# Wide cross attention of a two-layer decoder: keys and values folded into the weights, heads side by side, the norm inside the loop

## The chip, the cores and the metric

The kernel runs on one core of a Trainium2 chip. The metric is the device time of one execution in microseconds. Three runs of the kernel before took 2298.8, 2303.5 and 2313.93 us: median 2303.5 us.

## What is computed

Two decoder layers on x (4 batches, 512 tokens, 128 features), each with self attention, cross attention and experts, a layer norm behind each. The change is in the cross attention of the second layer, with 16 heads of width 64 over a context of 77 rows of 128 features for each batch:

```
q = einsum('bqm,mhd->bqhd', x, Wq) + bq
k = einsum('bkm,mhd->bkhd', ctx, Wk) + bk
v = einsum('bkm,mhd->bkhd', ctx, Wv) + bv
attn = softmax(einsum('bqhd,bkhd->bhqk', q / sqrt(64), k), axis=-1)
out  = einsum('bqhd,hdm->bqm', einsum('bhqk,bkhd->bqhd', attn, v), Wo) + bo
x = layernorm(x + out)
```

Everything here is float32.

## The kernel before, in words

The program is written by engine. Each function opens a block in which the engines run their own lists of instructions and wait on counting semaphores; between blocks all engines meet. Constants: P = 128, B = 4 batches, S = 512 tokens of a batch, QT = 4 tiles of 128 tokens in a batch, NT = 16 tiles in all, KC = 77 context rows, H = 16 heads, PAIRS = 8 pairs of heads. Lasting tiles are X (tokens on partitions), XT (its transpose, features on partitions) and CTT (the context transposed). PSUM has ps_s (four banks of 512 columns), ps_t (two), ps_v and ps_f (one each).

The stage named e has three parts.

- **Operands** (first block of `wide_cross_attention`). SP loads four weights of 512 KB and four biases; PE waits for all of them. For each pair of heads PE makes keys (L1685, 308 columns: 4 batches of 77) and half a batch of values (L1690, 512 columns); DVE writes them out with their biases (L1702 twice, L1707).
- **The loop** (second block), 32 turns: a batch and a pair of heads in each, for all 512 tokens. `project` (L1721) makes the queries, which ACT takes out (L1836); `score` (L1728) multiplies four token tiles by the keys of two heads side by side (154 columns); `lessen` on DVE takes maxima (L1785) and subtracts them (L1788); ACT takes the exponential (L1830); `norm` on DVE sums (L1795), inverts (L1797) and scales (L1799); `turn` on PE makes eight transposes of 77 columns (L1739), ACT takes them out (L1854); `weigh` (L1750) multiplies the values; DVE takes the heads out (L1807); `add` (L1758) multiplies by Wo and sums over the pairs in ps_f. The order on each engine is written out by hand. PE's turn is: score of the pair two ahead, turn, project three ahead, add of the pair before, weigh. DVE's turn is: lessen two ahead, norm one ahead, take the heads out. The first batch and the last are written out, the two between run in a hardware loop.
- **The norm** (`finish`, tag e). A block of its own: it transposes the output back to tokens (L948), adds X (L1008), takes statistics (L846, L849), POOL computes the inverse root (L857, L859), DVE applies it (L866), and PE and ACT rebuild XT (L959, L983).

The next stage's first instruction is a load of the router's weights. `lessen`, `take`, `turn` and `score` also name inner functions of other stages; those are not touched.

Of the kernel before, what the change touches and what calls it, by code (L numbers as in the profile page):

```python
# [5 lines left out]
F32 = mybir.dt.float32  # L6
# [5 lines left out]
P = 128  # L12
# [19 lines left out]
CLIP = 16  # L32
EPS = 1e-5
# [1595 lines left out]

def wide_cross_attention(c, tag, wq, bq, wk, bk, wv, bv, wo, bo, OT):  # L1630

    nc = c.nc
    with ExitStack() as own:
        WQ, WK, WV = (c.sb(f"{tag}_W{n}", [P, H * HD64], F32, own) for n in "qkv")
        WO = c.sb(f"{tag}_Wo", [P, PAIRS, P], F32, own)
        BQ = c.sb(f"{tag}_BQ", [P, PAIRS], F32, own)
        BK = c.sb(f"{tag}_BK", [P, PAIRS], F32, own)
        BV = c.sb(f"{tag}_BV", [KC, H * HD64], F32, own)
        BO = c.sb(f"{tag}_BO", [P, 1], F32, own)
        KB = c.sb(f"{tag}_KB", [P, PAIRS, B, 2, KC], F32, own)  # L1640
# [3 lines left out]
        SC = c.sb(f"{tag}_SC", [P, 2, 2 * QT, KC], F32, own)
        PR = c.sb(f"{tag}_PR", [P, 2, 2 * QT, KC], F32, own)
        PT = c.sb(f"{tag}_PT", [SROWS, 2, S], F32, own)
        CT = c.sb(f"{tag}_CT", [P, S], F32, own)
        M = c.sb(f"{tag}_M", [P, 2 * QT], F32, own)
        DEN = c.sb(f"{tag}_DEN", [P, 2 * QT], F32, own)
        RDEN = c.sb(f"{tag}_RDEN", [P, 2 * QT], F32, own)  # L1650
        (s_w, s_zero, s_scaled, s_kproj, s_kout, s_vproj, s_vout, s_vb, proj, q_out, scores, maxed, lessened, exped, summed,
         inverted, normed, turned, taken, products, heads_out, added, s_ot) = (
            c.sem(f"{tag}_{n}") for n in
            ("w", "zero", "scaled", "kproj", "kout", "vproj", "vout", "vb", "proj", "q_out", "scores", "maxed", "lessened",
             "exped", "summed", "inverted", "normed", "turned", "taken", "products", "heads_out", "added", "ot"))
        N_W = 16 * 8

        with nc.Block() as block:
            @block.sync
            def _(sp):  # L1660
                for dst, src in ((WQ, wq), (WK, wk), (WV, wv)):
                    sp.dma_start(dst[:, :], src.rearrange("m h d -> m (h d)")).then_inc(s_w, 16)
                sp.dma_start(WO[:, :, :], wo.rearrange("(g e) d n -> (e d) g n", e=2)).then_inc(s_w, 16)
                sp.dma_start(BQ[:, :], bq.rearrange("(g e) d -> (e d) g", e=2),
                             allow_slow_non_contiguous=True).then_inc(s_w, 16)
                sp.dma_start(BK[:, :], bk.rearrange("(g e) d -> (e d) g", e=2),
                             allow_slow_non_contiguous=True).then_inc(s_w, 16)
# [12 lines left out]
            def _(pe):  # L1680
                pe.wait_ge(s_w, N_W)
                for p in range(PAIRS):
                    if p >= 2:
                        pe.wait_ge(s_kout, 2 * (p - 1))
                    nc.tensor.matmul(c.ps_s[:, p % 2, 0:B * KC], WK[:, p * P:(p + 1) * P], c.CTT[:, :],  # L1685
                                     start=True, stop=True).then_inc(s_kproj, 1)
                    b, half = p // 2, p % 2
                    if p >= 2:
                        pe.wait_ge(s_vout, p - 1)
                    nc.tensor.matmul(c.ps_t[0:KC, half, :], c.CTT[:, b * KC:(b + 1) * KC], WV[:, half * 512:(half + 1) * 512],  # L1690
                                     start=True, stop=True).then_inc(s_vproj, 1)
# [510 lines left out]
```

## Time and profile before

| what | us |
|---|---|
| median of three runs (lowest, highest) | 2303.5 (2298.8, 2313.93) |
| the profiled execution, first to last instruction | 2295.7 |
| stage e: operands | 27.6 |
| stage e: loop | 167.9 |
| stage e: norm function | 16.7 |
| PE, DVE, ACT, POOL busy over the span | 1810.9, 1433.0, 1046.3, 119.8 |

The span is measured inside one profiled execution; no separate duration is given for that execution, and the runs' times, taken on other executions, are 3.1 to 18.2 us above it. The table is read by stage: only the three rows on stage e belong to code that changes. Engine times say how long an engine had an instruction in it; a matmul's end is modelled, so overlapping matmuls are shown longer than the steps between them. A float32 matmul stands as two entries, a float32 transpose as one. PEclk is TensorE's granted clock: 1.00 is 2.4 GHz, 0.50 is 1.2 GHz.

### The profile page before, as it was taken

The page shows a single profiled execution, that of the slowest core. Times are in us where ns is not written, and L with a number is a line of the kernel's source. Part 1 is how long each engine was busy: PE and PEld are TensorE (multiplying, and loading weights), DVE is VectorE, ACT ScalarE, POOL GpSimd, SP SyncE. Part 2 cuts the span into 40 slices and gives each one's busy share as a digit, 9 for nine tenths or more (in the row PEclk, how much of TensorE's full clock was granted, in tenths as well). Part 3 has the DMA queues.
Part 4 walks back from the last instruction along what each step waited for, and adds up shares of the span by engine and source line. Part 5 has one row for each costly group of instructions (what it writes and reads, how often), then busy time and mean ns, then how long its engine had stood idle before and what let it go on. Part 6 is the DMA issues. An engine that isn't in the chain of part 4 may idle for free. (4 is left out here: it accounts for less than half of the span.)

```text
span 2295.7 us, 33834 instructions
## 1 busy us (share of the span) xinstructions
PE 1810.9 (79%) x9702; PEld 1004.4 (44%) x9702; DVE 1433.0 (62%) x4803; ACT 1046.3 (46%) x1972; POOL 119.8 (5%) x244
## 2 busy tenths in 40 slices
PE   3288774684169559699985999999999959998997
PEld 2144442453013223477762444444444425555664
DVE  7398886565368446333336777777767757875445
ACT  3288881471026346243432555666665513441221
POOL 2000003001000000100001000000000020000000
PEclk7599996796569779699997999999999978997999
DMA  1543200510531230100001000000000010000000
GB/s 57 80 44 37 28 0 22 72 21 22 90 35 18 24 42 1 31 10 19 26 2 37 1 1 1 1 1 1 0 1 1 1 43 1 0 1 21 15 21 25
DMA packets 56587, 48.93 MB, mean 21 GB/s; under 512 B 11742, under 2 KB 51922, under 8 KB 56479
## 3 DMA queue, kind: packets, MB, share of 16 engines
q1 hardware_dynamic: 56479, 47.67, 12.8%
q8 instruction: 47, 0.77, 0.1%
q14 instruction: 61, 0.50, 0.1%
HBM read 38.54 MB, written 8.91 MB: 21 GB/s over the span
## 5 line engine op out<-in xcount | busy, mean ns | idle before, releaser
L1431 PE MATMUL ps_s<-d_KZ,d_Q 128*128 128x512 f32 x512 | 265.4, 601 | 16.2 <-issue 6.8
L1579 ACT ACTIVATE d_PR<-d_PR,d_NM 128x512 f32<-128x512 f32 x256 | 184.7, 721 | 190.0 <-DVE d_NM L1510 189.5
L556 DVE TENSOR_REDUCE c_NM<-ps_t 128x1 f32<-128x512 f32 x256 | 170.0, 689 | 96.8 <-PE ps_t L436 95.1
L1506 DVE CUSTOM_DVE_ANT_0 d_PR<-ps_s,d_BH 128x512 f32<-128x512 f32 x256 | 176.3, 689 | 61.6 <-PE ps_t L1439 44.7
L2116 DVE SCALAR_TENSOR_TENSOR X<-ps_t,GATE,X 128x128 f32<-128x128 f32 x272 | 76.6, 345 | 183.7 <-PE ps_t L2041 183.7
L436 PE MATMUL ps_t<-KX,QX 96*128 (+1 forms) x256 | 108.1, 427 | 105.3 <-DVE c_IB L574 46.2
L618 ACT ACTIVATE c_PT<-ps_s 128x1024 f32<-128x1024 f32 x128 | 130.3, 1023 | 126.8 <-PE ps_s L459 124.8
L1439 PEld LDWEIGHTS ps_t<-ident,d_PR 128*128 128x128 f32 x1024 | 121.4, 141 | 150.6 <-issue 132.4
L1586 ACT ACTIVATE d_PT<-ps_t 128x512 f32<-128x512 f32 x256 | 149.6, 585 | 50.7 <-PE ps_t L1439 49.1
L761 ACT ACTIVATE a_PR<-a_PR,a_NM 128x128 f32<-128x128 f32 (+3 forms) x256 | 129.8, 555 | 78.5 <-DVE a_NM L742 78.5
L1439 PE MATMUL ps_t<-ident,d_PR 128*128 128x128 f32 x1024 | 156.5, 276 | 10.0 <-ACT d_PT L1586 8.1
L671 PE MATMUL ps_t<-ident,a_PR 128*128 128x128 f32 x640 | 115.8, 290 | 46.7 <-ACT a_PT L685 37.7
L2078 ACT ACTIVATE f_HT<-ps_s,f_BE 128x512 f32<-128x512 f32 x128 | 87.7, 687 | 127.8 <-PE ps_s L2031 127.1
L2031 PE MATMUL ps_s<-XT,g_W 128*128 128x512 f32 x288 | 132.6, 604 | 1.1 <-DVE g_HT L2095 1.1
L1518 DVE TENSOR_SCALAR d_PR<-d_PR,d_RDEN 128x512 f32<-128x512 f32 x256 | 124.7, 487 | 9.0
L2041 PEld LDWEIGHTS ps_t<-f_W,f_HT 128*128 128x128 f32 x1024 | 119.2, 192 | 14.8 <-issue 14.6
L1451 PE MATMUL ps_v<-d_PT,d_VB 128*64 128x512 f32 x512 | 116.9, 598 | 5.6 <-ACT d_PT L1586 4.8
L2041 PE MATMUL ps_t<-f_W,f_HT 128*128 128x128 f32 x1024 | 119.3, 275 | 0.0
L2031 PE MATMUL ps_s<-XT,f_W 128*128 128x512 f32 x256 | 116.6, 599 | 0.0
L671 PEld LDWEIGHTS ps_t<-ident,a_PR 128*128 128x128 f32 x640 | 70.6, 142 | 96.1 <-ACT a_PT L685 48.0
L2076 ACT ACTIVATE g_GT<-ps_s 128x512 f32<-128x512 f32 x72 | 43.0, 597 | 141.8 <-PE ps_s L2031 141.8
L436 PEld LDWEIGHTS ps_t<-KX,QX 96*128 (+1 forms) x256 | 25.0, 98 | 184.3 <-issue 105.3
(306 smaller groups left out, 3182.2 us busy)
## 6 DMA issues: line engine op xcount, KB each, us to landing
QX<-split_parts SPq DMA_DIRECT2D x108, 128.0 KB
KX<-split_parts SPq DMA_DIRECT2D x72, 128.0 KB
f_W<-in_L_ffn_w SPq DMA_DIRECT2D x16, 256.0 KB, 3.1
split_parts<-a_PARTS SPq DMA_DIRECT2D x8, 384.0 KB, 10.4
split_parts<-c_PARTS SPq DMA_DIRECT2D x8, 384.0 KB, 10.8
g_W<-in_L_ffn_w SPq DMA_DIRECT2D x24, 128.0 KB, 2.2
split_parts<-b_PARTS SPq DMA_DIRECT2D x4, 384.0 KB, 10.5
X<-in_x SPq DMA_DIRECT2D x4, 256.0 KB
```

Source lines behind the costliest of these rows:

```text
L436: nc.tensor.matmul(c.ps_t[:, i % 2, :], QX[0:SROWS, bass.ds(head, 1), qt * P:(qt + 1) * P], KX[0:SROWS, bass.ds(head, 1), :], start=True, ...
L556: nc.vector.tensor_reduce(NM[:, qt, j:j + 1], c.ps_t[:, i % 2, :], AX.X, ALU.max, negate=True).then_inc(maxed, 1)
L618: nc.scalar.activation(PT[:, half, j, :, :], c.ps_s[:, 2 * (j % 2):2 * (j % 2) + 2, :], ACT.Exp).then_inc(exped, 1)
L671: last = nc.tensor.transpose(c.ps_t[:, qt % 2, kt * P:(kt + 1) * P], PR[:, j % 2, qt, kt * P:(kt + 1) * P], c.ident[:, :])
L761: nc.scalar.activation(PR[:, j % 2, qt, 0:k], PR[:, j % 2, qt, 0:k], ACT.Exp, bias=NM[:, j % 2, qt:qt + 1]).then_inc(exped, 1)
L1431: nc.tensor.matmul(c.ps_s[:, qt % 2, :], Q[:, p % 2, qt * P:(qt + 1) * P], KZ[:, p % 2, i % 2, :], start=True, stop=True).then_inc(scores, 1)
L1439: mm = nc.tensor.transpose(c.ps_t[:, qt % 2, kt * P:(kt + 1) * P], PR[:, i % 2, qt, kt * P:(kt + 1) * P], c.ident[:, :])
L1506: nc.vector.tensor_tensor_reduce(out=PR[:, h % 2, qt, :], in0=c.ps_s[:, qt % 2, :], in1=BH[:, h, S - P - qt * P:2 * S - P - qt * P], scale ...
L1579: nc.scalar.activation(PR[:, h % 2, qt, :], PR[:, h % 2, qt, :], ACT.Exp, bias=NM[:, h % 2, qt:qt + 1], accum_out=DEN[:, h % 2, qt:qt + 1] ...
L1586: nc.scalar.activation(PT[:, i // 2 % 2, i % 2, :, qt * P:(qt + 1) * P], c.ps_t[:, qt % 2, :].rearrange("p (k q) -> p k q", q=P), ACT.Copy ...
L2031: nc.tensor.matmul(c.ps_s[:, ch, :], W[:, (ch % CH) * P:(ch % CH + 1) * P], c.XT[:, b * S:(b + 1) * S], start=True, stop=True).then_inc(s_ ...
L2041: mm = nc.tensor.matmul(c.ps_t[:, b % 2, q * P:(q + 1) * P], HT[:, b % 2, ch, q * P:(q + 1) * P], W2[i][:, ch, :], start=(ch == 0), stop=( ...
```

## The change

`wide_cross_attention` and `finish` for stage e are replaced by three functions. For each head h, `wide_operands` folds Wq[h] and the keys into A[h] = Wq[h] K[h]^T / 8 (128 features by 308 context rows), and the values and Wo[h] into U (context rows by 128 features). `flat_cross` then multiplies XT by A directly, with no queries, and the probabilities by U, with no product with Wo. The query bias becomes a row CP that is added by a second matmul, in three bfloat16 parts against ones.

A turn is now half of a token tile's heads: 8 heads of 77 columns side by side, 616 columns padded to 640, which makes five transposes of 128 columns. There are again 32 turns, all written out. The exponential is taken in place. The scaling by 1/sum is `normalise` on GpSimd, L1853 of the new kernel. The output bias is added to X on GpSimd before the loop. The output of a tile is added to X by DVE (L1982), and statistics, scaling and the new XT of a batch are done within the turns of the next batch; the last batch's follow the loop.

The diff, cut; removed lines are those of the function shown above.

```diff
-def wide_cross_attention(c, tag, wq, bq, wk, bk, wv, bv, wo, bo, OT):
...
+def flat_operand_tiles(c, tag, ctx):
+    A = c.sb(f"{tag}_A", [P, B, H, KC], F32, ctx)
+    CP = c.sb(f"{tag}_CP", [NPART, H, B, KC], BF16, ctx)
+    U = c.sb(f"{tag}_U", [P, B, 2 * CHUNKS, P], F32, ctx)
+    return A, CP, U
...
+def wide_operands(c, tag, wq, bq, wk, bk, wv, bv, wo, A, CP, U):
...
+                for dst, src in ((WK, wk), (WV, wv), (WQ, wq)):
                     sp.dma_start(dst[:, :], src.rearrange("m h d -> m (h d)")).then_inc(s_w, 16)
                 sp.dma_start(WO[:, :, :], wo.rearrange("(g e) d n -> (e d) g n", e=2)).then_inc(s_w, 16)
+                for dst, src in ((BQ, bq), (BK, bk), (BV, bv)):
+                    sp.dma_start(dst[:, :], pairs(src), allow_slow_non_contiguous=True).then_inc(s_w, 16)
...
+                for p in range(PAIRS):
+                    if p >= 2:
+                        pe.wait_ge(s_kout, p - 1)
+                    nc.tensor.matmul(c.ps_s[:, p % 2, 0:K2], WK[:, p * P:(p + 1) * P], c.CTT[:, :],
+                                     start=True, stop=True).then_inc(s_k, 1)
+                    if p >= 2:
                         pe.wait_ge(s_vout, p - 1)
+                    nc.tensor.matmul(c.ps_s[:, 2 + p % 2, 0:K2], WV[:, p * P:(p + 1) * P], c.CTT[:, :],
+                                     start=True, stop=True).then_inc(s_v, 1)
+                    mm = nc.tensor.transpose(c.ps_t[:, p // 4, (p % 4) * P:(p % 4 + 1) * P], WQ[:, p * P:(p + 1) * P],
+                                             c.ident[:, :])
+                    if p % 4 == 3:
+                        mm.then_inc(s_wqt, 1)
+                pe.wait_ge(s_bq, 2)
+                pe.wait_ge(s_kout, PAIRS)
+                for p in range(PAIRS):
+                    mm = nc.tensor.matmul(c.ps_f[0:H, 0:K2], BQH[:, p * H:(p + 1) * H], KT[:, p, :],
+                                          start=(p == 0), stop=(p == PAIRS - 1))
+                mm.then_inc(s_c, 1)
+                pe.wait_ge(s_wqtout, 2)
+                pe.wait_ge(s_vout, PAIRS)
+                for p in range(PAIRS):
+                    if p >= 2:
+                        pe.wait_ge(s_aout, 2 * (p - 1))
+                    for e in range(2):
+                        r = slice(e * HD64, (e + 1) * HD64)
+                        mm = nc.tensor.matmul(scored(2 * p + e), WQT[r, p, :], KT[r, p, :], start=True, stop=True)
+                    mm.then_inc(s_a, 1)
+                    if p == 1:
+                        pe.wait_ge(s_split, 1)
+                    if p >= 2:
+                        pe.wait_ge(s_uout, 2 * (p - 1))
+                    for e in range(2):
+                        r = slice(e * HD64, (e + 1) * HD64)
+                        mm = nc.tensor.matmul(valued(2 * p + e), WO[r, p, :], VT[r, p, :], start=True, stop=True)
+                    mm.then_inc(s_u, 1)
+                pe.wait_ge(s_aout, H)
+                pe.wait_ge(s_zero, 2)
+                for g in range(B * 2):
+                    b, half = g // 2, g % 2
+                    if g == 0:
+                        pe.wait_ge(s_uout, H)
+                    if g >= 2:
+                        pe.wait_ge(s_tout, g - 1)
+                    for i in range(CHUNKS):
+                        mm = nc.tensor.transpose(c.ps_s[:, 2 * (g % 2) + i // 4, (i % 4) * P:(i % 4 + 1) * P],
+                                                 UT[:, b, half, i * P:(i + 1) * P], c.ident[:, :])
+                    mm.then_inc(s_t, 1)
...
+                for h in range(H):
+                    act.wait_ge(s_a, h // 2 + 1)
+                    nc.scalar.activation(A[:, :, h, :], scored(h).rearrange("p (b k) -> p b k", b=B),
+                                         ACT.Copy).then_inc(s_aout, 1)
+                for g in range(B * 2):
+                    act.wait_ge(s_t, g + 1)
+                    nc.scalar.activation(U[:, g // 2, (g % 2) * CHUNKS:(g % 2 + 1) * CHUNKS, :].rearrange("p i d -> p (i d)"),
+                                         c.ps_s[:, 2 * (g % 2):2 * (g % 2) + 2, :].rearrange("p a n -> p (a n)")[:, 0:W],
+                                         ACT.Copy).then_inc(s_tout, 1)
...
+                for h in range(H):
+                    dve.wait_ge(s_u, h // 2 + 1)
+                    nc.vector.tensor_copy(UT[:, :, h // 8, (h % 8) * KC:(h % 8 + 1) * KC],
+                                          valued(h).rearrange("p (b k) -> p b k", b=B)).then_inc(s_uout, 1)
...
+def flat_cross(c, tag, A, CP, U, bo, pre=None):
...
+                pool.wait_ge(s_w, n_w)
+                for b in range(B):
+                    x = c.X[:, b * QT:(b + 1) * QT, :]
+                    nc.gpsimd.tensor_tensor(x, x, BO[:, :].rearrange("p (a d) -> p a d", a=1).broadcast_to([P, QT, P]),
+                                            ALU.add).then_inc(s_bias, 1)
...
+                def normalise(h):
+                    pool.wait_ge(inverted, h + 1)
+                    nc.gpsimd.tensor_tensor(
+                        heads(PR[:, h % RING, 0:HH * KC]), heads(PR[:, h % RING, 0:HH * KC]),
+                        RDEN[:, h % 2, :].rearrange("p (h a) -> p h a", a=1).broadcast_to([P, HH, KC]),
+                        ALU.mult).then_inc(normed, 1)
+                for h in range(HALVES):
+                    normalise(h)
+                    if h % (2 * QT) == 3 and h > 3:
+                        for k in range(norms):
+                            rstd((h // (2 * QT) - 1) * norms + k)
+                for k in range(norms):
+                    rstd((B - 1) * norms + k)
...
+                def score(h):
+                    t, half = h // 2, h % 2
+                    b = t // QT
+                    if h >= 2:
+                        pe.wait_ge(lessened, h - 1)
+                    for q in range(2):
+                        g = slice(half * HH + 4 * q, half * HH + 4 * q + 4)
+                        dst = c.ps_s[:, 2 * (h % 2) + q, 0:4 * KC]
+                        nc.tensor.matmul(dst, c.XT[:, t * P:(t + 1) * P], A[:, b, g, :].rearrange("p h k -> p (h k)"),
+                                         start=True, stop=False)
+                        mm = nc.tensor.matmul(dst, ONES[:, :], CP[:, g, b, :], start=False, stop=True)
                     mm.then_inc(scores, 1)
+                def turn(h):
+                    pe.wait_ge(normed, h + 1)
+                    if h >= 1:
+                        pe.wait_ge(taken, h)
+                    for i in range(CHUNKS):
+                        mm = nc.tensor.transpose(c.ps_t[:, i // 4, (i % 4) * P:(i % 4 + 1) * P],
+                                                 PR[:, h % RING, i * P:(i + 1) * P], c.ident[:, :])
                     mm.then_inc(turned, 1)
+                def weigh(h):
+                    t, half = h // 2, h % 2
+                    pe.wait_ge(taken, h + 1)
+                    if half == 0 and t >= 2:
+                        pe.wait_ge(summed_x, t - 1)
+                    for i in range(CHUNKS):
+                        mm = nc.tensor.matmul(output(t), PT[:, h % 2, i * P:(i + 1) * P], U[:, t // QT, half * CHUNKS + i, :],
+                                              start=(half == 0 and i == 0), stop=(half == 1 and i == CHUNKS - 1))
+                    mm.then_inc(weighed, 1)
+                def back(b):
+                    pe.wait_ge(s_n, QT * (b + 1))
+                    for i in range(QT):
+                        src = c.X[:, b * QT + i, :] if pre is None else R2[:, i, :]
+                        mm = nc.tensor.transpose(c.ps_t[:, 0, i * P:(i + 1) * P], src, c.ident[:, :])
+                    mm.then_inc(s_back, 1)
+                pe.wait_ge(s_ones, 1)
+                pe.wait_ge(s_pad, 1)
+                score(0)
+                score(1)
+                for h in range(HALVES):
+                    if h % (2 * QT) == 6 and h > 6:
+                        pe.wait_ge(taken, h)
+                        back(h // (2 * QT) - 1)
+                        pe.wait_ge(s_xt, h // (2 * QT))
+                    turn(h)
+                    if h + 2 < HALVES:
+                        score(h + 2)
+                    weigh(h)
+                back(B - 1)
...
+                def exp(h):
+                    act.wait_ge(lessened, h + 1)
+                    nc.scalar.activation(PR[:, h % RING, 0:HH * KC], PR[:, h % RING, 0:HH * KC], ACT.Exp).then_inc(exped, 1)
+                def take(h):
+                    act.wait_ge(turned, h + 1)
+                    if h >= 2:
+                        act.wait_ge(weighed, h - 1)
+                    nc.scalar.activation(PT[:, h % 2, :], c.ps_t[:, :, :].rearrange("p a n -> p (a n)")[:, 0:W],
+                                         ACT.Copy).then_inc(taken, 1)
...
+                for h in range(HALVES):
+                    if h % (2 * QT) == 6 and h > 6:
+                        columns(h // (2 * QT) - 1)
+                    take(h)
+                    if h + 2 < HALVES:
+                        exp(h + 2)
...
+                def lessen(h):
+                    dve.wait_ge(scores, h + 1)
+                    m = M[:, h % 2, :].rearrange("p (a m) -> p a m", a=2)
+                    nc.vector.reduce_max(m, score_banks(h), AX.X).then_inc(maxed, 1)
+                    dve.wait_ge(maxed, h + 1)
+                    if h >= RING:
+                        dve.wait_ge(turned, h - RING + 1)
+                    nc.vector.tensor_tensor(
+                        PR[:, h % RING, 0:HH * KC].rearrange("p (a m k) -> p a m k", a=2, k=KC), score_banks(h),
+                        M[:, h % 2, :].rearrange("p (a m b) -> p a m b", a=2, b=1).broadcast_to([P, 2, 4, KC]),
+                        ALU.subtract).then_inc(lessened, 1)
+                def total(h):
+                    dve.wait_ge(exped, h + 1)
+                    nc.vector.reduce_sum(DEN[:, h % 2, :], heads(PR[:, h % RING, 0:HH * KC]), AX.X).then_inc(summed, 1)
+                    dve.wait_ge(summed, h + 1)
+                    if h >= 2:
+                        dve.wait_ge(normed, h - 1)
+                    nc.vector.reciprocal(RDEN[:, h % 2, :], DEN[:, h % 2, :]).then_inc(inverted, 1)
+                def add(t):
+                    dve.wait_ge(weighed, 2 * t + 2)
+                    if t == 0:
+                        dve.wait_ge(s_bias, B)
+                    nc.vector.tensor_tensor(c.X[:, t, :], c.X[:, t, :], output(t), ALU.add).then_inc(summed_x, 1)
...
+                lessen(0)
+                lessen(1)
+                total(0)
+                for h in range(HALVES):
+                    if h + 2 < HALVES:
+                        lessen(h + 2)
+                    if h + 1 < HALVES:
+                        total(h + 1)
+                    if h % 2 == 0 and h >= 2:
+                        add(h // 2 - 1)
+                    if h > 3 and h % (2 * QT) in (2, 3, 4, 5)[:1 + norms] and h >= 2 * QT:
+                        layer(h // (2 * QT) - 1, h % (2 * QT) - 2)
+                add(NT - 1)
+                for step in range(1 + norms):
+                    layer(B - 1, step)
+                done.wait(dve)
...
-            wide_cross_attention(c, "e", *(a[f"L1_xattn_{n}"] for n in ("Wq", "bq", "Wk", "bk", "Wv", "bv", "Wo", "bo")), OT)
-            finish(c, "e", "dm", OT=OT)
+            A, CP, U = flat_operand_tiles(c, "e", own)
+            wide_operands(c, "e", *(a[f"L1_xattn_{n}"] for n in ("Wq", "bq", "Wk", "bk", "Wv", "bv", "Wo")), A, CP, U)
+            flat_cross(c, "e", A, CP, U, a["L1_xattn_bo"])
         with ExitStack() as own:
             GATE = c.sb("GATE1", [P, NT, NE + 1], F32, own)
```

The order on PE, where the scores are made in the loop. Before (a stretch of the hardware loop; L1728 score, L1739 turn, L1721 project, L1758 add, L1750 weigh):

```order
L1739 MATMUL ps_t<-ident,e_PR 77x128 x8
L1721 MATMUL ps_s<-XT,e_Wq 128x512
L1758 MATMUL ps_f<-e_CT,e_Wo 128x512
L1750 MATMUL ps_v<-e_PT,e_VB 64x512 x2
L1728 MATMUL ps_s<-e_KB,e_Q 128x154 x4
L1739 MATMUL ps_t<-ident,e_PR 77x128 x8
```

The same place in the changed kernel (L1886 turn, L1876 and L1878 score, L1896 weigh):

```order
L1886 MATMUL ps_t<-ident,e_PR 128x128 x5
L1876 MATMUL ps_s<-e_A,XT 128x308
L1878 MATMUL ps_s<-e_CP,e_ONES 128x308
L1876 MATMUL ps_s<-e_A,XT 128x308
L1878 MATMUL ps_s<-e_CP,e_ONES 128x308
L1896 MATMUL ps_v<-e_U,e_PT 128x128 x5
L1886 MATMUL ps_t<-ident,e_PR 128x128 x5
```

The score of two turns ahead stood before the turn's transposes; now it stands behind them, and ahead of the weighing.

The order on DVE in the loop. Before (L1785 and L1788 lessen, L1795 to L1799 norm, L1807 heads out):

```order
L1785 TENSOR_REDUCE e_M<-ps_s 128x8
L1788 TENSOR_TENSOR e_SC<-ps_s,e_M 128x616
L1795 TENSOR_REDUCE e_DEN<-e_PR 128x8
L1797 RECIPROCAL e_RDEN<-e_DEN 128x8
L1799 TENSOR_TENSOR e_PR<-e_PR,e_RDEN 128x616
L1807 COPY e_CT<-ps_v 128x512
```

Now (L1961 and L1965 lessen, L1972 and L1976 total, L1982 add of a finished tile, every second turn):

```order
L1961 TENSOR_REDUCE e_M<-ps_s 128x8
L1965 TENSOR_TENSOR e_PR<-ps_s,e_M 128x616
L1972 TENSOR_REDUCE e_DEN<-e_PR 128x8
L1976 RECIPROCAL e_RDEN<-e_DEN 128x8
L1961 TENSOR_REDUCE e_M<-ps_s 128x8
L1965 TENSOR_TENSOR e_PR<-ps_s,e_M 128x616
L1972 TENSOR_REDUCE e_DEN<-e_PR 128x8
L1976 RECIPROCAL e_RDEN<-e_DEN 128x8
L1982 TENSOR_TENSOR X<-X,ps_v 128x128
```

The scaling has left DVE, and the copy of 512 columns has become an addition of 128; maxima and subtraction of a later turn still come ahead of the sums of an earlier one.

## Rows read from the trace of the kernel before

**Rows 1.** Windows by stage: length, busy us per engine (count), PEclk, DMA share, GB/s.
```profile
1867.90:1895.50 27.60, 14.03 (x32) 5.70 (x32) 13.74 (x25) 0.00 (x0) 8.65 (x3) 0.73 0.31 88
1895.50:2063.40 167.90, 162.05 (x768) 92.85 (x768) 130.05 (x196) 72.65 (x100) 0.00 (x0) 0.96 0.00 1
2063.40:2080.10 16.70, 6.70 (x32) 4.42 (x32) 11.77 (x52) 3.05 (x5) 5.06 (x8) 0.71 0.00 0
```

**Rows 2.** Timeline, one turn of the loop: start us, us, instruction, [idle before <-releaser].
```profile
1977.41 1.31 PE L1728 MATMUL ps_s<-e_KB,e_Q 128*128 x8
...
1978.57 1.04 PE L1739 MATMUL ps_t<-ident,e_PR 128*77 128x128 f32 x8
1978.77 0.80 DVE L1785 TENSOR_REDUCE e_M<-ps_s 128x8 f32<-128x616 f32 x1 [0.54 <-PE ps_s L1728]
...
1979.69 0.80 DVE L1788 TENSOR_TENSOR e_SC<-ps_s,e_M 128x616 f32<-128x616 f32 x1
...
1980.40 0.78 DVE L1795 TENSOR_REDUCE e_DEN<-e_PR 128x8 f32<-128x616 f32 x1
...
1981.22 0.20 DVE L1797 RECIPROCAL e_RDEN<-e_DEN 128x8 f32<-128x8 f32 x1
...
1981.25 1.08 PE L1750 MATMUL ps_v<-e_PT,e_VB 96*64 96x512 f32 x4
1981.46 0.80 DVE L1799 TENSOR_TENSOR e_PR<-e_PR,e_RDEN 128x616 f32<-128x616 f32 x1
...
1982.26 1.31 PE L1728 MATMUL ps_s<-e_KB,e_Q 128*128 x8
```

**Rows 3.** Timeline, the stage's weights and operands.
```profile
1867.90 0.33 SPq L1662 DMA_DIRECT2D e_Wq<-in_L_xattn_Wq  x1
...
1870.38 3.83 SPq L1666 DMA_DIRECT2D e_BK<-in_L_xattn_bk  x1
...
1878.85 1.40 PE L1685 MATMUL ps_s<-CTT,e_Wk 128*128 128x308 f32 x2 [11.84 <-DMA e_BO<-in_L_xattn_bo]
...
1880.36 1.11 DVE L1702 TENSOR_SCALAR e_KB<-ps_s,e_BK 64x308 f32<-64x308 f32 x2 [1.35 <-PE ps_s L1685]
...
1883.63 0.68 PE L1685 MATMUL ps_s<-CTT,e_Wk 128*128 128x308 f32 x2
...
1894.53 0.69 DVE L1707 TENSOR_TENSOR e_VA<-ps_t,e_BV 77x512 f32<-77x512 f32 x1
```

**Rows 4.** Timeline, end of the loop and the separate norm function.
```profile
2065.35 0.69 DVE L1008 TENSOR_TENSOR e_fR<-X,ps_s 128x512 f32<-128x512 f32 x1 [3.19 <-PE ps_s L948]
...
2066.98 0.38 DVE L849 BATCH_NORM_AGGREGATE e_fMV<-e_fST 128x2 f32<-128x6 f32 x4
...
2067.45 0.23 POOL L857 TENSOR_SCALAR e_fRS<-e_fMV 128x4 f32<-128x4 f32 x1 [190.77 <-DVE e_fMV L849]
...
2071.32 0.60 ACT L983 ACTIVATE XT<-ps_t 128x512 f32<-128x512 f32 x1 [7.26 <-PE ps_t L959]
...
2079.28 0.60 ACT L983 ACTIVATE XT<-ps_t 128x512 f32<-128x512 f32 x1 [0.99 <-PE ps_t L959]
```

**Rows 5.** Groups by line on POOL, whole span: op, shapes xcount | busy us, mean ns.
```profile
L365 POOL COPY VG<-c_VN 128x32 f32 x56 | 11.4, 209 | 278.5 <-PE ps_v L476 278.5
...
L1673 POOL MEMSET e_KB<- 128x4928 f32 x1 | 4.2, 4204 | 3.2 <-POOLq L903 3.2
...
L367 POOL COPY VG<-b_VB 96x8 f32 x14 | 2.6, 186 | 81.5 <-PE ps_v L1236 81.5
```

**Rows 6.** Timeline, PE early in the loop.
```profile
1907.64 0.59 PE L1728 MATMUL ps_s<-e_KB,e_Q 128*128 128x154 f32 x1 [2.91 <-DVE e_SC L1788]
```

**Rows 7.** Windows early in the loop, columns as in the first group.
```profile
1903.50:1906.50 3.00, 1.24 (x8) 1.00 (x8) 2.34 (x4) 1.13 (x2) 0.00 (x0) 1.00 0.00 0
1907.00:1913.00 6.00, 5.36 (x18) 4.25 (x18) 3.32 (x6) 1.94 (x3) 0.00 (x0) 0.50 0.00 0
1914.00:1926.00 12.00, 12.00 (x67) 7.49 (x64) 9.22 (x14) 4.57 (x7) 0.00 (x0) 1.00 0.01 1
```

More of the change, by code:

```diff
@@ L32 @@
 CLIP = 16
+CHUNKS = 5
 EPS = 1e-5
@@ L1644, in wide_cross_attention @@
[L1644 to L1655, printed above, removed]
@@ L1709, in ahead @@
-        def ahead(b, p, k):
-            return (b, p + k) if p + k < PAIRS else (b + 1, p + k - PAIRS)
-        def more(p, k, last):
-            return not last or p + k < PAIRS
-        with nc.Block() as block:
+                split = Chain(s_split)
+                dve.wait_ge(s_w, 16 * 7)
+                dve.wait_ge(s_zero, 1)
+                for e in range(2):
+                    r = slice(e * HD64, (e + 1) * HD64)
+                    nc.vector.tensor_scalar(BQH[r, e::H + 2], BQ[r, :], ISQ64, None, ALU.mult).then_inc(s_bq, 1)
@@ L1754, in add @@
-                def add(b, p):
-                    wait(pe, heads_out, b * PAIRS + p + 1)
-                    if p == 0:
-                        wait(pe, s_ot, b)
-                    nc.tensor.matmul(c.ps_f[:, :], WO[:, p, :], CT[:, :], start=(p == 0), stop=(p == PAIRS - 1)).then_inc(added, 1)
-                def batch(b, first, last):
-                    if first:
-                        project(b, 0)
-                        project(b, 1)
-                        score(b, 0)
-                        project(b, 2)
-                        score(b, 1)
-                    for p in range(PAIRS):
-                        if more(p, 2, last):
-                            score(*ahead(b, p, 2))
-                        turn(b, p)
-                        if more(p, 3, last):
-                            project(*ahead(b, p, 3))
-                        if not (first and p == 0):
-                            add(*((b, p - 1) if p else (b - 1, PAIRS - 1)))
-                        weigh(b, p)
@@ L1803, in take_heads @@
-                def take_heads(b, p):
-                    n = b * PAIRS + p
-                    dve.wait_ge(products, n + 1)
-                    dve.wait_ge(added, n)
-                    nc.vector.tensor_copy(CT[:, :], c.ps_v[:, :]).then_inc(heads_out, 1)
-                def batch(b, first, last):
-                    wait(dve, products, b * PAIRS)
-                    nc.vector.tensor_copy(VB[:, :], VA[:, bass.ds(b, 1), :].rearrange("p a n -> p (a n)")).then_inc(s_vb, 1)
-                    if first:
-                        lessen(b, 0)
-                        norm(b, 0)
-                        lessen(b, 1)
-                    for p in range(PAIRS):
-                        if more(p, 2, last):
-                            lessen(*ahead(b, p, 2))
-                        if more(p, 1, last):
-                            norm(*ahead(b, p, 1))
-                        take_heads(b, p)
```

262 lines of the change are left out of this document (133 added, 129 removed).

## The prediction

> **What bounds the kernel now.** I read the windows by stage first, because one stage of several changes. Stage e takes 27.6 us for its operands, 167.9 for its loop and 16.7 for its norm function, 212.2 us in all [rows 1]. In the loop PE is busy 162.05 of 167.9 us, DVE 130.05, ACT 72.65, POOL not at all: PE bounds it. In the operands and the norm nothing is full; there the order of waits counts. Then I read one turn in the timeline: from score to score 4.85 us (1977.41 to 1982.26) [rows 2]. The reader should see in it that DVE's maxima start while PE is still in its transposes: score stands ahead of the transposes on PE, so DVE works on a later pair of heads while PE turns an earlier one. Over 32 turns, 4.85 us make 155 us; the rest of the loop is its start.
>
> **What the change takes away.** Queries, the product with Wo, the copy of the heads (DVE), the copy of queries (ACT), the scaling on DVE, and the separate norm function. Of a turn's work PE keeps five transposes of eight, 5/8 of 1.04 = 0.65 us; the score, two float32 products of 308 columns at 0.68 each from start to end [rows 3], 1.36 us; two bfloat16 products of 308 columns; and the weighing, five products of 128 columns, about 1.1 us (640 columns by 0.68/308, less overlapping ends). The trace has no bfloat16 product of this form: it costs at least nothing and at most one of the two entries of the float32 one, 0.34 us; I take 0.1 for both beyond the overlap, nearer to nothing since the ends shown overlap. Together 3.2 us for PE. DVE keeps 0.80 + 0.80 + 0.78 + 0.20 [rows 2], half of an addition of 128 columns and an eighth of a batch's norm, about 3.1 us. Against 4.85 that looks like a gain of 1.7 us a turn. It is not the sum, for what follows.
>
> **The order makes a chain.** PE now issues turn(h), score(h+2), weigh(h). turn(h) waits for POOL's scaling of h, which waits for DVE's total(h). DVE issues total(h) behind lessen(h+1), which waits for score(h+1), which PE issues behind turn(h-1). So turn(h-1), score(h+1), lessen(h+1), total(h), normalise(h), turn(h) follow each other with nothing beside them but the weighing and the ACT copies. Queued behind the waiting turn on PE is the score of two turns ahead, and DVE waits for that: the two stages of prefetch buy nothing. Before, score of two ahead waited for no transposes.
>
> The price of a turn, at 2.4 GHz: transposes 0.65; scores 1.36 + 0.1 = 1.46; DVE from the start of the maxima to the point where the scaling can start 2.69 (1978.77 to 1981.46) [rows 2]; scaling p; handovers PE to DVE and POOL to PE, 0.15 together (DVE to POOL took 0.09, from 2067.36 to 2067.45 [rows 4]).
>
> **The scaling on GpSimd, p.** No POOL row has two inputs of this length. A copy of 32 columns takes 209 ns, of 8 columns 186 [rows 5]: 0.96 ns a column over a fixed 0.18 us. For 616 columns one input is 0.77 us. With two inputs I take twice the cost per column, 1.36 us. Below, the memset, which reads nothing, costs 4204/4928 = 0.85 ns a column: 0.53 and a tenth for the start, 0.63 us. Above, three times the copy's slope: 1.95 us. The copy is the nearest row, since it reads and writes as the scaling does; DVE's 0.80 for the same work is another engine's. The Trainium skill, "GPSIMD Engine Reference", section "Elementwise — side-by-side cycle accounting", speaks against this move: two inputs cost GpSimd 1.96 times what they cost VectorE. By that, an estimate of 1.96 x 0.80 = 1.57 us would make the sum 6 us longer; no run here shows it yet.
>
> With p = 1.36 a turn is 0.65 + 1.46 + 2.69 + 1.36 + 0.15 = **6.3 us** at 2.4 GHz, and PE is idle for some 3 us of it. At 1.2 GHz transposes and scores double, which gives 8.4 us; DVE, ACT and POOL do not change.
>
> **The clock.** In the first turns of the loop before, PE stood idle 2.91 us for DVE [rows 6]; from 1903.5 to 1906.5 it was busy 1.24 us and the clock was 1.00, and from 1907 to 1913 it was at 0.50 although PE was busy 5.36 of 6 us; unbroken work followed and it was 1.00 again from 1914 on [rows 7]. The new turn contains such an idle stretch every time, and behind it come just the transposes and scores that lie on the chain; the rise comes, if at all, in the weighing, which does not. I take the middle of the two levels, 7.35 us a turn. The Trainium skill, "TensorE: Matmul & The Clock Gate", section "What's actually happening", puts it so that the slow level is the default and activity releases it; the trace agrees, and the rule's extreme, a loop that never leaves 1.2 GHz, is a rival below.
>
> **Loop and norm.** Start: two scores at the low clock 5.8, lessen(1) and total(0) 2.7, scaling and handover 1.5: 10.0 us. The four bias additions on POOL and the load of the bias lie beside that. 30 turns x 7.35 = 220.5. The last turn has no score ahead: 1.5. Behind it the last transposes, copy and weighing, 2.5, and one batch's norm, from the addition to the end of the new XT: 2065.35 to 2071.92 = 6.6 [rows 4]. Sum 241.1 us against 167.9 + 16.7 = 184.6 [rows 1]: **+56.5**. The norms of the first three batches I cost at nothing: DVE is idle for more than 3 us of a turn and POOL for some 6; if the chain were gone they would cost DVE about 0.3 us a turn.
>
> **Operands.** Before, 10.95 us until the last bias landed (1867.90 to 1878.85), then 16.7 us of products [rows 3]. Now: loads 13.0, since a third bias is scattered by columns, which cost SP 3.83 us to issue for one such, where a row load stood; I take 2 of 0 to 4 us. Keys, values and turned Wq, 8 x 1.2 = 9.6, and 1.7 for the start at half clock, where the first product shows 1.40 for 0.68: 11.3. The bias row, eight products in turn and the first split, 5.1. A and U: 32 products of half height. If the two halves of a pair run side by side, DVE's two copies set it, 1.11 a pair as the two of 308 columns [rows 3]: 8.9 us. If not, PE does, with four at 0.51: 16.4. The nearest row is the weighing before, whose two column halves run together (four entries of 512 columns in 1.08 us [rows 2]), so I take 8.9. Turning U: eight groups at 0.75 for ACT's 640 columns (512 take 0.60 [rows 4]) and a start: 6.8. Handover 0.8. Sum 45.9 against 27.6: **+18.3**, from 16 to 28.
>
> **The sum.** 2295.7 + 56.5 + 18.3 = 2370.5 us for the profiled execution's span. The median of the runs lies 7.8 us above the span of before; with the same around it the median is **2378 us**, 3.2% slower.
>
> **Rivals.**
> - Clock at 1.00 all through. For it: the idle stretch is only half of a turn, and weighing joins on to transposes and scores. Against it: [rows 6, 7]. 6.3 us a turn: 2378 - 30 x 1.05 = 2346 us.
> - Clock at 0.50 all through. For it: 5.36 busy of 6 us did not raise it at once [rows 7]. Against it: then PE works some 6 us of 8.4 without a break, where those 6 us held pauses. 2378 + 31 = 2410 us.
> - A cheap scaling, 0.63 us, together with the high clock: 5.6 us a turn, 2324 us, within 1%. Needs the lower bound of two costs.
> - The other side: the chain does not close, and DVE's 3.1 us set the turn. The place is DVE's wait for the score behind total(h): it would need score(h+1) done before turn(h-1) has been released, which the order forbids. 2378 - 30 x 4.25 = 2250 us, faster. The point at which it decides: the operands, start and end take 45.9 + 20.6 us, so the stage equals its old 212.2 us at 4.86 us a turn.
> - The change doing less than it says: GpSimd's scaling is certainly in the list, so this only concerns the halves of A and U; serial halves add 7.5 us to any case.
>
> **Chances.** Alternating clock 0.50, high 0.27, low 0.13, cheap and high 0.05, no chain 0.05. The range takes in the first three with the scaling's ends (18 us either way) trimmed: 2325 to 2415 us. A measurement of this kernel tells about 1% from no change, 23 us. Slower by more 0.90, within 0.05, faster 0.05.
>
> **What would show it.** In the changed kernel's profile: DVE's maxima waiting for PE's scores in nearly every turn; PE's transposes waiting for the scaling about 3 us; 6.3 to 8.4 us between two groups of transposes; 1.36 us for the scaling; PEclk between 0.5 and 1.0 in the loop; the operands 44 to 56 us long; about 10 us between the last scaling and the router's load. The forecast fails if turns are below 5.6 us, if the scaling is far outside 0.6 to 2 us, or if the idle stretch leaves the clock alone.

## The result, and the profile after

The changed kernel takes **2385.4 us** (median; 2377.0 to 2395.0), the kernel before 2302.9 us in the same comparison: 1.035 times as long, 95% interval 1.032 to 1.039. The forecast was 2378 us and slower. The profiled execution of the new kernel has a span of 2393.2 us and is its slowest run, so its stages are compared by their lengths and not by the span. Of the page of the new kernel:

```profile
span 2393.2 us, 33578 instructions
...
PE 1842.1 (77%) x9665; PEld 1041.4 (44%) x9718; DVE 1385.4 (58%) x4754; ACT 1035.7 (43%) x1970; POOL 155.9 (7%) x281
...
PEclk7699995896588989899969999999999865766999
```

The last row is the granted clock in 40 slices: it stands at 5 to 7 tenths in the four slices of this stage's loop. The windows by stage, to be held against [rows 1] (length; busy us, with counts, of PE, PEld, DVE, ACT and POOL; PEclk, DMA share, GB/s):

```profile
1876.00:1920.00 44.00, 30.52 (x160) 19.88 (x160) 13.79 (x32) 16.29 (x34) 0.55 (x3) 0.83 0.18 49
1920.00:2175.00 255.00, 192.57 (x688) 124.75 (x688) 94.18 (x192) 47.86 (x68) 49.03 (x46) 0.63 0.00 1
```

From the first weight load to the router's load, stage e took 212.2 us before and takes 299.1 now, +86.9: operands 44.0 against 27.6, loop with norms 255.1 against 167.9 + 16.7. The other 10.6 us by which this execution's span is longer lie in stages that the change doesn't touch (8.1 ahead, 2.5 behind); in the kernels of the experiments, which are the same up to this stage, it starts anywhere from 1866 to 1878 us. DVE has only 94.18 us of work in the loop, where it had 130.05 and 11.77, and PE's 192.57 is more than its old 162.05 only because its clock stood at 0.63 on average instead of 0.96: the same 688 entries take 125.1 us at a clock of 0.92 in the kernel with the total ahead of lessening, below (1918.0 to 2060.7).

One turn at the high clock (start us, us, instruction, [idle before <-releaser]), in place of [rows 2]:

```profile
2040.13 0.74 PE L1886 MATMUL ps_t<-ident,e_PR 128*128 128x128 f32 x5 [1.34 <-ACT XT L1939]
...
2040.70 0.69 PE L1876 MATMUL ps_s<-e_A,XT 128*128 128x308 f32 x2
...
2042.27 0.30 PE L1878 MATMUL ps_s<-e_CP,e_ONES 3*128 3x308 bf16 x1
...
2042.50 1.38 PE L1896 MATMUL ps_f<-e_U,e_PT 128*128 128x128 f32 x10
2042.61 0.80 DVE L1961 TENSOR_REDUCE e_M<-ps_s 128x8 f32<-128x616 f32 x1 [3.87 <-PE ps_s L1878]
...
2045.26 1.22 POOL L1853 TENSOR_TENSOR e_PR<-e_PR,e_RDEN 128x616 f32<-128x616 f32 x1 [5.23 <-DVE e_RDEN L1976]
2046.53 0.53 PEld L1886 LDWEIGHTS ps_t<-ident,e_PR 128*128 128x128 f32 x5 [2.83 <-POOL e_PR L1853]
2046.53 0.77 PE L1886 MATMUL ps_t<-ident,e_PR 128*128 128x128 f32 x5 [2.65 <-POOL e_PR L1853]
```

Read it as a ladder: transposes (2040.13), score (2040.70 to 2042.57), DVE (2042.61), scaling (2045.26), transposes (2046.53). Each starts where the one before ends, and the brackets tell the same: every engine waits for the one ahead, PE 2.65 us, DVE 3.87, POOL 5.23. (The first line names ACT's XT as what ended its wait, since a new batch starts there; XT was copied by 2039.43, and the scaling ended at 2040.03, so this wait too is for the scaling.) Before, DVE's maxima had begun beside PE's transposes. At the low clock a turn is longer:

```profile
1938.08 1.33 PE L1886 MATMUL ps_t<-ident,e_PR 128*128 128x128 f32 x5 [1.52 <-POOL e_PR L1853]
...
1942.54 0.80 DVE L1961 TENSOR_REDUCE e_M<-ps_s 128x8 f32<-128x616 f32 x1 [5.80 <-PE ps_s L1878]
...
1945.19 1.22 POOL L1853 TENSOR_TENSOR e_PR<-e_PR,e_RDEN 128x616 f32<-128x616 f32 x1 [7.16 <-DVE e_RDEN L1976]
...
1946.46 1.33 PE L1886 MATMUL ps_t<-ident,e_PR 128*128 128x128 f32 x5 [1.53 <-POOL e_PR L1853]
```

From 1938.08 to 1946.46 are 8.38 us; transposes and score take 4.46 instead of 2.48 and nothing else changes. DVE's maxima wait for the score 32 times, every turn (us in all, times, the longest):

```profile
DVE e_M L1961 <- PE ps_s L1878: 153.0, 32, 9.7
```

### The profile page after: what moved, and what is told of

Its sections match the earlier page's. It is cut to its first block and busy times, and to the rows that moved or that the text cites. A ratio compares the mean times of both kernels' runs of the same rounds, so it can differ in the third digit from the quotient of the medians.

```text
span 2393.2 us, 33578 instructions
## 1 busy us (share of the span) xinstructions
PE 1842.1 (77%) x9665; PEld 1041.4 (44%) x9718; DVE 1385.4 (58%) x4754; ACT 1035.7 (43%) x1970; POOL 155.9 (7%) x281
## 5 line engine op out<-in xcount | busy, mean ns | idle before, releaser
L1961 DVE TENSOR_REDUCE e_M<-ps_s 128x8 f32<-128x616 f32 x32 | 25.6, 800 | 153.0 <-PE ps_s L1878 153.0
```

## The experiments

The comparisons are against the kernel before (2302.0 us for the first four, 2300.7 for the next four, 2302.6 for the last). "The stage" is the length from the first weight load to the router's load, 212.2 us before and 299.1 in the change. Lengths of turns are those within a batch; where a new batch starts, a turn can be longer.

**Score ahead of the transposes, on PE.**

```diff
-                    turn(h)
                     if h + 2 < HALVES:
                         score(h + 2)
+                    turn(h)
```

> Only PE's order in the loop changes: score(h+2) stands ahead of turn(h). Theory (the order closes a chain through turn, score, lessen, total and scaling): the chain then runs over two turns, weighing and the wait for ACT's copy now on it; two turns cost about 2.4 (transposes, copy, weighing) + 1.5 (score) + 2.7 (DVE) + 1.4 (scaling and handovers) = 8.0 us, so 4.0 to 4.3 us a turn instead of 7.67, and the clock stays up since PE works 3.2 of them: 2385 - 30 x 3.5 = 2275 to 2285 us, below the kernel before. Rival (GpSimd's scaling or the engines' own work bounds the turn): no engine has less to do, so 2375 to 2390 us.

Measured: 2295.4 us, ratio 0.998 (0.996 to 0.999); the stage 207.0 us; a turn 4.57 us. The timeline:

```profile
1992.40 0.70 ACT L1932 ACTIVATE e_PT<-ps_t 128x640 f32<-128x640 f32 x1 [2.89 <-PE ps_t L1886]
...
1993.16 1.38 PE L1896 MATMUL ps_f<-e_U,e_PT 128*128 128x128 f32 x10 [0.79 <-ACT e_PT L1932]
...
1994.36 1.22 POOL L1853 TENSOR_TENSOR e_PR<-e_PR,e_RDEN 128x616 f32<-128x616 f32 x1 [3.36 <-DVE e_RDEN L1976]
1994.38 0.68 PE L1876 MATMUL ps_s<-e_A,XT 128*128 128x308 f32 x2
...
1996.17 0.77 PE L1886 MATMUL ps_t<-ident,e_PR 128*128 128x128 f32 x5
```

The chain is gone: the scaling (1994.36 to 1995.58) is over before PE wants it at 1996.17. Two lines swapped take 92 us off the stage. It stays above the 2275 to 2285 us that were expected since PE's own row now sets the turn: it stands idle 0.79 us for ACT's copy before each weighing, and the score takes 1.8 us.

**Total ahead of lessening, on DVE.**

```diff
+                    if h + 1 < HALVES:
+                        total(h + 1)
                     if h + 2 < HALVES:
                         lessen(h + 2)
-                    if h + 1 < HALVES:
-                        total(h + 1)
```

> Only DVE's order changes: total(h+1) stands ahead of lessen(h+2). Chain theory: the scaling of h+1 runs beside score(h+2), the chain is turn, score, lessen, exponential, total, scaling over two turns, 0.65 + 1.5 + 1.6 + 0.7 + 1.0 + 1.4 = 6.9 us for two; DVE has 3.1 us of work and about 0.8 of waiting for the exponential in each turn, so about 4.0 to 4.5 us a turn: 2275 to 2290 us. Rival (work of the engines): 2375 to 2390 us.

Measured: 2276.7 us, 0.989 (0.987 to 0.990); the stage 186.7 us; turns of 3.56 and 3.74 us.

```profile
1992.76 1.22 POOL L1853 TENSOR_TENSOR e_PR<-e_PR,e_RDEN 128x616 f32<-128x616 f32 x1 [2.34 <-DVE e_RDEN L1976]
...
1992.88 1.38 PE L1896 MATMUL ps_v<-e_U,e_PT 128*128 128x128 f32 x10
1992.98 0.80 DVE L1961 TENSOR_REDUCE e_M<-ps_s 128x8 f32<-128x616 f32 x1 [0.30 <-PE ps_s L1878]
...
1994.09 0.71 PE L1886 MATMUL ps_t<-ident,e_PR 128*128 128x128 f32 x5
...
1995.40 0.80 DVE L1972 TENSOR_REDUCE e_DEN<-e_PR 128x8 f32<-128x616 f32 x1 [0.59 <-ACT e_PR L1926]
```

The scaling now runs beside the weighing and PE has no gap at 1994.09; DVE waits 0.30 us for the score and not 3.87. So the same chain can be opened on either engine, and DVE's side is the better one: PE's order stays transposes, score, weighing, so that the score runs while ACT makes its copy (1991.53 to 1992.22) and PE finds it done at 1992.88. The turns are below the 4.0 to 4.5 us expected; the median is within the 2275 to 2290 expected, since turns that hold a part of a norm take longer, two of them 5.43 us.

**The scaling on DVE, orders as in the change.**

```diff
-                    nc.gpsimd.tensor_tensor(
...
                     nc.vector.reciprocal(RDEN[:, h % 2, :], DEN[:, h % 2, :]).then_inc(inverted, 1)
+                    dve.wait_ge(inverted, h + 1)
+                    nc.vector.tensor_tensor(
+                        heads(PR[:, h % RING, 0:HH * KC]), heads(PR[:, h % RING, 0:HH * KC]),
...
```

> The scaling is back on DVE, behind the reciprocal; all orders stay. Chain theory: the chain loses 1.22 + 0.1 us and gains 0.80, so 7.95 instead of 8.38 us a turn at the low clock and 6.0 instead of 6.4 at the high one, minus 13 us: about 2372 us, still 3% above the kernel before. Rival (GpSimd's scaling is what makes the change slow): most of the 82 us go, 2300 to 2320 us.

Measured: 2362.5 us, 1.026 (1.024 to 1.029); the stage 270.8 us; turns of 5.97 us at the high clock, 7.55 and 7.92 with the low one in them.

```profile
2043.98 0.80 DVE L1970 TENSOR_TENSOR e_PR<-e_PR,e_RDEN 128x616 f32<-128x616 f32 x1
...
2044.84 0.77 PE L1878 MATMUL ps_t<-ident,e_PR 128*128 128x128 f32 x5 [1.30 <-DVE e_PR L1970]
...
2047.35 0.80 DVE L1953 TENSOR_REDUCE e_M<-ps_s 128x8 f32<-128x616 f32 x1 [2.37 <-PE ps_s L1870]
```

DVE still waits for the score behind the transposes. In the chain GpSimd costs 28 us of the stage and 23 of the median, where 13 were expected. Its longer instruction and the handover make 0.46 us a turn at either clock (6.43 against 5.97, 8.38 against 7.92), 14 us; most of the rest are turns at the low clock, of which this kernel has fewer: its mean turn is 6.85 us against 7.67. GpSimd is not what makes the kernel slow.

**PE kept busy.** This kernel does work that nobody needs: five more products of 308 columns behind each weighing, where PE was idle.

```diff
                     weigh(h)
+                    for _ in range(5):
+                        nc.tensor.matmul(c.ps_t[:, 1, P:P + B * KC], c.ident[:, :], c.CTT[:, :], start=True, stop=True)
```

> PE makes five extra float32 products of 308 columns behind each weighing, into columns that nobody reads (about 2.6 us at 2.4 GHz, in a wait of some 3 us). Added work, same results. Theory (the alternating clock costs 7.67 - 6.43 us a turn): PE has no long idle stretch any more, the clock is 1.00 after the first turns, 6.4 us a turn, minus 30 to 37 us: 2350 to 2355 us. Rival (the clock follows something else, or the extra products delay the turn): same or slower, 2385 to 2430 us.

Measured: 2355.6 us, 1.024 (1.022 to 1.027); the stage 268.2 us. Windows and one turn:

```profile
1935.00:1940.00 5.00, 5.00 (x25) 3.35 (x24) 2.50 (x4) 1.40 (x2) 0.67 (x1) 1.00 0.02 3
1955.00:1960.00 5.00, 4.95 (x24) 3.34 (x25) 2.65 (x5) 0.72 (x1) 1.22 (x1) 1.00 0.00 0
2085.00:2090.00 5.00, 5.00 (x25) 3.36 (x24) 2.66 (x5) 1.39 (x2) 0.68 (x1) 1.00 0.00 0
```

```profile
2041.72 2.76 PE L1921 MATMUL ps_t<-CTT,ident 128*128 128x308 f32 x10
...
2044.53 0.76 PE L1886 MATMUL ps_t<-ident,e_PR 128*128 128x128 f32 x5
...
2047.03 0.80 DVE L1963 TENSOR_REDUCE e_M<-ps_s 128x8 f32<-128x616 f32 x1 [3.86 <-PE ps_s L1878]
```

More work, and 31 us less: after the first two turns the clock is 1.00, and a turn takes 6.43 us (7.50 in two turns in which a batch changes, where the added products hold up PE's transposes of X). DVE waits as long as ever. Of the change's +86.9 us in the stage the clock is at least 31.

**Total first, and the scaling on DVE:** both edits shown above together.

> DVE's order as in the kernel with total ahead of lessen (2276.7 us), and the scaling back on DVE behind the reciprocal. Theory: with the chain open, DVE's own work decides; it rises from 3.65 us a turn by 0.80, in part beside PE, to 4.4 to 4.7 us, plus 24 to 32 us: 2300 to 2308 us, no better than the kernel before; GpSimd's slower scaling is the cheaper place then. Rival (GpSimd costs also here, as in the chain, where DVE's scaling saved 23 us): 2255 to 2270 us.

Measured: 2290.7 us, 0.995 (0.993 to 0.998); the stage 201.1 us, turns 4.19 us; lower than the 2300 to 2308 expected, but 14 us of the stage behind the same order with GpSimd. With the chain open the move to GpSimd is right: it takes 0.80 us of work a turn off DVE, and the turn is 0.54 us shorter.

**Norms taken out of the loop again,** from the kernel with total first; rstd, back, columns and layer leave the loop:

```diff
-                    if h > 3 and h % (2 * QT) in (2, 3, 4, 5)[:1 + norms] and h >= 2 * QT:
-                        layer(h // (2 * QT) - 1, h % (2 * QT) - 2)
...
+            finish(c, "e", "x")
```

> As the kernel with total ahead of lessen (2276.7 us), but with statistics, scaling and the new XT in a norm function of their own behind the loop, as before. Theory: norms in the turns are hidden; apart they cost a block's start and four batches in turn, about 15 us, against the last batch's 6.6 us: plus 8 to 10 us, 2285 us. Rival (in the turns they hold DVE and PE up as much, 2 us where a batch turns over, three times): within 2274 to 2280 us.

Measured: 2275.1 us, 0.989 (0.985 to 0.992); the stage 185.1 us. About 2285 us were expected; the rival, no difference, came true, and the norm inside the loop gains nothing over the separate function. What it costs there is seen in the kernel with total first, at a change of batches:

```profile
1981.36 0.60 PE L1904 MATMUL ps_t<-ident,X 128*128 128x128 f32 x4
...
1982.53 0.58 ACT L1939 ACTIVATE XT<-ps_t 128x512 f32<-128x512 f32 x1
...
1983.17 0.76 PE L1886 MATMUL ps_t<-ident,e_PR 128*128 128x128 f32 x5 [1.21 <-ACT XT L1939]
```

PE turns the new X and then waits for ACT to copy it, behind an exponential; this turn takes 5.4 us.

**Bias products grouped,** from the kernel with total first:

```diff
                         nc.tensor.matmul(dst, c.XT[:, t * P:(t + 1) * P], A[:, b, g, :].rearrange("p h k -> p (h k)"),
                                          start=True, stop=False)
+                    for q in range(2):
+                        g = slice(half * HH + 4 * q, half * HH + 4 * q + 4)
+                        dst = c.ps_s[:, 2 * (h % 2) + q, 0:4 * KC]
                         mm = nc.tensor.matmul(dst, ONES[:, :], CP[:, g, b, :], start=False, stop=True)
```

> As the kernel with total ahead of lessen (2276.7 us), but PE makes both float32 products of a score first and then both bias products, so that each stationary operand stands twice in a row. Theory: the score takes 1.8 us where its columns need 1.3, because each bias product waits for its own operand between two float32 ones; grouped, PE saves 0.2 to 0.4 us of a turn that it fills: minus 5 to 12 us, 2265 to 2272 us. Rival (the bias products cost by themselves, wherever they stand): 2275 to 2278 us.

Measured: **2270.3 us**, 0.986 (0.982 to 0.990), the lowest median of all; the stage 181.1 us, turns of 3.31 and 3.69 us. The interval overlaps that of the kernel it starts from (0.987 to 0.990), so the gain rests on the traces: 5.6 us of the stage.

```profile
1991.08 1.20 PE L1876 MATMUL ps_s<-e_A,XT 128*128 128x308 f32 x4
...
1992.21 0.43 PE L1881 MATMUL ps_s<-e_CP,e_ONES 3*128 3x308 bf16 x2
1992.58 1.19 PEld L1899 LDWEIGHTS ps_v<-e_U,e_PT 128*128 128x128 f32 x10 [0.26 <-ACT e_PT L1935]
```

From 1991.08 to 1992.64 the score takes 1.56 us instead of 1.87, so the rival, that these products cost the same wherever they stand, falls.

**Weighing one turn later,** from the kernel with the score first:

```diff
-                    weigh(h)
+                    if h >= 1:
+                        weigh(h - 1)
+                weigh(HALVES - 1)
```

> As the kernel with the score ahead of the transposes (2295.4 us, 4.58 us a turn, in each of which PE waited 0.8 to 1.0 us for ACT's copy), but PE weighs the turn before behind the transposes. Theory: that wait goes; a turn is PE's 3.6 to 3.7 us: minus 27 us, 2266 to 2270 us. Rival (the chain over two turns is itself 4.5 us): 2290 to 2296 us.

Measured: 2276.5 us, 0.988 (0.984 to 0.992); the stage 183.5 us, turns of 3.52 and 4.03 us. PE's 0.79 us wait for ACT is gone, and with it 23.5 us of the stage; the median is 19 us lower and lies 7 above the expectation. In every second turn PE waits for the scaling again:

```profile
1999.08 0.80 DVE L1963 TENSOR_REDUCE e_M<-ps_s 128x8 f32<-128x616 f32 x1 [0.79 <-PE ps_s L1878]
...
1999.48 0.77 PE L1886 MATMUL ps_t<-ident,e_PR 128*128 128x128 f32 x5 [0.44 <-POOL e_PR L1853]
```

**Grouped bias products and norms apart,** both edits together:

> The two small gains together on the kernel with total ahead of lessen: bias products grouped (its stage took 181.0 us in the trace against 186.7) and the norm in a function of its own (185.2). If they add, the stage takes 179 to 180 us and the run 2267 to 2270 us; if the norm apart only traded one wait for another that the faster loop does not have, the stage takes 181 to 184 us, 2270 to 2274 us, the same as with the bias products grouped alone.

Measured: 2273.2 us, 0.987 (0.985 to 0.990); the stage 178.7 us. Its interval overlaps that of the grouped products alone: the norm's place doesn't show in the time, though the stage is 2.3 us shorter, as short as was expected if both gains add.

## Why the prediction was right, and where its terms were off

The mechanism was the one forecast: a chain through PE, DVE and POOL that PE's order and DVE's order close together, and that opens when either is turned round. Both were tried, and either alone takes the kernel to or below the time before (0.998 and 0.989). By its steps, in us of the profiled execution:

| step | forecast | measured |
|---|---|---|
| operands | 45.9 | 44.0 |
| start of the loop | 10.0 | 9.7 (1920.0 to 1929.71) |
| 30 turns | 220.5 (7.35 each) | 230.1 (7.67 each; 1929.71 to 2159.85) |
| last turn | 1.5 | 4.4 (to 2164.24) |
| last transposes to router's load | 9.1 | 10.9 (to 2175.10) |
| stage | 287.0 | 299.1 |

- **Turn at 2.4 GHz:** 6.3 forecast, 6.40 to 6.44 measured, by errors that cancel. The score is 1.87 us and not 1.46: a product of three bfloat16 rows takes 0.30 us at its end and stands between float32 ones, and I had priced both such products together at 0.1. Against these 0.41 us stand four terms that I had too high, 0.32 us together: the scaling is 1.22 and not 1.36, DVE's part 2.65 and not 2.69, the transposes up to the score's start 0.57 and not 0.65, the handovers 0.09 and not 0.15. That the sum is within 0.1 us is luck.
- **The scaling on GpSimd.** All 32 took 1216 or 1217 ns, over DVE's 0.80 for the same work 1.52 times:

```profile
L1853 POOL TENSOR_TENSOR e_PR<-e_PR,e_RDEN x32: 1216/1217/1217, 1928.4 to 2159.7; 128x616 f32<-128x616 f32 x32
```

  The measurement decides against the Trainium skill here ("GPSIMD Engine Reference", "Elementwise — side-by-side cycle accounting"): its 1.96, given there for an addition of 2048 columns, would have made 1.57 us, an estimate.
- **The clock.** It did alternate. Windows of the change:

```profile
1935.00:1940.00 5.00, 3.48 (x15) 2.72 (x13) 1.70 (x3) 1.27 (x2) 1.22 (x1) 0.50 0.00 0
1940.00:1945.00 5.00, 4.93 (x15) 2.91 (x14) 2.40 (x4) 0.87 (x2) 0.00 (x0) 0.50 0.00 0
...
1955.00:1960.00 5.00, 3.63 (x21) 2.31 (x20) 2.50 (x4) 1.42 (x2) 0.00 (x0) 1.00 0.00 0
2085.00:2090.00 5.00, 3.27 (x19) 1.95 (x17) 2.68 (x6) 1.42 (x2) 0.35 (x1) 1.00 0.00 0
2135.00:2140.00 5.00, 4.13 (x11) 2.16 (x11) 0.84 (x7) 0.70 (x1) 2.09 (x3) 0.50 0.00 0
```

  The mean turn lies nearer to the low end (8.38) than to the high one (6.43); by these two, 0.64 of the way. The middle was a choice. Of this term's error, (7.67 - 7.35) x 30 = 9.6 us, about 8 come from it, since the middle of the two measured levels is 7.41; the rest is the price of a turn. The rival with a high clock all through was 2346 us; the kernel with PE kept busy is that rival made real, at 2355.6.
- **Last turn and tail:** 2.9 and 1.8 us too low. The last score is gone, but the weighing of turn 30 stands before the last transposes, and at the low clock it takes 2.50 us, as the last one does (the norm behind it was 0.6 us shorter than forecast, 6.0 for 6.6):

```profile
2164.24 1.27 PE L1886 MATMUL ps_t<-ident,e_PR 128*128 128x128 f32 x5
2165.55 0.70 ACT L1932 ACTIVATE e_PT<-ps_t 128x640 f32<-128x640 f32 x1 [3.65 <-PE ps_t L1886]
...
2166.30 2.50 PE L1896 MATMUL ps_f<-e_U,e_PT 128*128 128x128 f32 x10 [0.79 <-ACT e_PT L1932]
2168.84 0.29 DVE L1982 TENSOR_TENSOR X<-X,ps_f 128x128 f32<-128x128 f32 x1 [9.34 <-PE ps_f L1896]
```

- **Operands.** The halves of A and U run side by side, four entries in 0.69 us, so the serial rival (+7.5) fell. The loads took 9.8 us and not 13.0: of the three scattered biases only one was slow to issue, and no single size can be carried from one to the next. The rest of the operands took 34.2 us for 32.9:

```profile
1877.82 1.13 SPq L1677 DMA_DIRECT2D e_Bq<-in_L_xattn_bq  x1
1879.00 3.29 SPq L1677 DMA_DIRECT2D e_Bk<-in_L_xattn_bk  x1
1882.33 1.36 SPq L1677 DMA_DIRECT2D e_Bv<-in_L_xattn_bv  x1
1885.84 0.50 PEld L1694 LDWEIGHTS ps_s<-CTT,e_Wk 128*128 128x128 f32 x2 [11.11 <-DMA e_Bv<-in_L_xattn_bv]
...
1903.39 0.69 PE L1717 MATMUL ps_s<-e_KT,e_WQT 64*128 64x308 f32 x4
```

- **From span to median.** I had set the median 7.8 us above the span, as before. The stage grew by 86.9 in the profiled execution, 12 more than forecast, but that execution is the slowest of its kernel, and the medians differ by 82.5. Nor does a run's time lie 7.8 us above its own span: the change's profiled execution took 2394.99 us and has a span of 2393.2, 1.8 less, and every other run shows the same 1.7 to 1.8. So the profiled execution of the kernel before, with its span of 2295.7, took some 2297.5 us (an estimate), 6 us less than its median. Part of the close hit, 2378 against 2385.4, is that.
- **Norms inside the loop** I costed at nothing. In the change the chain hides them: in the turn at 2040.13 XT is ready 0.60 us before the scaling is, and PE starts 0.10 us after the scaling. With the chain open they are no gain, as the kernel with the norms apart shows.

Still open: why the clock is high in one stretch of turns and low in the next, with the same work in each, and why the three bias loads differ.

## What to carry to other kernels

A prefetch counts only if no engine issues it behind a wait that its own result has to feed: follow one item's chain through all the engines' orders, and look for the step that stands in line behind a later item's. When such a chain closes, less work on the busiest engine buys nothing, and the engine that now idles may lose its clock too. Ask of work moved to a slower engine whether it lies in the chain: the same slower instruction, by 0.42 us a turn, cost 28 us of the stage inside it, in part through the clock, and outside it the move saved 14.

## What the runs showed of the hardware

- With PE idle 1.5 to 2.65 us in nearly every turn, the granted clock fell to 0.50 for several turns and came back to 1.00 for others, with no change in the work. Filling the gaps with useless products kept it at 1.00 and took 31 us off the stage.
- A product with three rows of bfloat16 is not cheap because it is small: 308 columns took 0.30 us to its end. Two of them put behind both float32 products, and not between, saved 0.31 us a score and 5.6 us of the stage.
- GpSimd did an elementwise product of 616 columns with a broadcast second input in 1.217 us in every one of 32, and needed about 1.5 times what DVE did.
